# Perceiver block on one core: keys stacked ahead of the output's write, tail weights in five groups, three tail stages at earlier steps, a tanh gate and Newton norms

## The reference

```python
x = x + xattn(layernorm(x), ctx_1024)   # 16 heads of 16, softmax over 4096 keys, projections Wq Wk Wv Wh
x = x + attn(layernorm(x))              # causal linear attention: q, k normalised per head of 16,
                                        # exp features (2 nodes of 32), output projection Wout
x = x + ffn(layernorm(x))               # h = silu(x @ wg.T) * (x @ wu.T); h @ wd.T; hidden 768
# the int32 weights wg, wu, wd are scaled by 1/127
# head norm: x / max(norm(x), 1e-12); layernorm: (x - mean) / sqrt(var + 1e-5)
```

## Time and profile before

| | before |
|---|---|
| median of 3 runs | 1024.28 us (1021.52 to 1024.69) |
| the profiled execution | 1023.58 us |
| its span, first to last instruction | 1021.9 us |
| PE busy | 891.8 us, 87% |
| ACT busy | 546.9 us, 54% |
| DVE busy | 497.6 us, 49% |
| POOL busy | 111.9 us, 11% |
| DMA moved | 118.00 MB, mean 115 GB/s |
| mean granted TensorE clock | 0.958 |
| part of the span before the last scores | 904 us |

### The profile page before, as it was taken

The page is one execution under the profiler, slowest core; times in us unless marked ns, Lnnn a source line. Parts: engine busy times, 40 slices in busy tenths (PEclk is TensorE's granted clock), DMA queues, the critical chain, the costliest instruction groups (busy, mean ns, idle before and its releaser), DMA issues.

```text
span 1021.9 us, 20838 instructions
## 1 busy us (share of the span) xinstructions
PE 891.8 (87%) x8819; PEld 619.7 (61%) x8819; DVE 497.6 (49%) x831; ACT 546.9 (54%) x597; POOL 111.9 (11%) x132
## 2 busy tenths in 40 slices
PE   5699699977999898898899898989899999977865
PEld 4566466645666666665566665665566666656654
DVE  6523135553544346764544345765454445614546
ACT  6177477755565655646465655646466566820101
POOL 1042000000231100000140100000041000004210
PEclk9799899999999999999899999999899999999798
DMA  6898998796866666377866666386967565120000
GB/s 173 147 198 234 154 150 182 146 165 87 173 125 118 111 115 114 101 116 114 187 111 118 107 121 119 89 135 106 180 105 128 103 114 102 14 42 1 1 1 13
DMA packets 59282, 118.00 MB, mean 115 GB/s; under 512 B 23152, under 2 KB 30320, under 8 KB 55728
## 3 DMA queue, kind: packets, MB, share of 16 engines
q1 hardware_dynamic: 57392, 112.22, 60.1%
q0 software_dynamic: 1792, 4.40, 1.5%
HBM read 78.84 MB, written 37.75 MB: 114 GB/s over the span
## 4 chain that ended last, share of the span: by engine, by line
PE 59%; DVE 12%; DMA 11%; issue 6%; ACT 5%; SPq 3%; DVEq 2%; POOL 2%; POOLq 0%; ACTq 0%
PE ps_o L712 16%; PE ps_s L724 12%; PE ps_p L563 7%; PE ps_p L530 7%; DMA kstack<-kscr 7%; ACT probs L993 4%; PE ps_a L656 3%; DVE kfeat L1238 2%; SPq L376 2%; PE ps_a L682 2%; PE ps_a L650 2%; DMA kscr<-kparts 2%; DMA qstack<-qscr 2%; PE ps_a L669 2%; PE ps_a L593 1%
## 5 line engine op out<-in xcount | busy, mean ns | idle before, releaser
L993 ACT ACTIVATE probs<-ps_s 128x1024 f32<-128x1024 f32 x512 | 495.6, 1024 | 289.6 <-PE ps_s L724 266.7
L712 PE MATMUL ps_o<-probs,values 128*17 128x256 f32 x4096 | 258.5, 388 | 0.0
L724 PE MATMUL ps_s<-qstack,kstack 64*128 64x256 f32 x2048 | 206.3, 315 | 56.5 <-DMA kstack<-kscr 34.0
L724 PEld LDWEIGHTS ps_s<-qstack,kstack 64*128 64x128 f32 x2048 | 145.0, 191 | 160.9 <-ACT probs L993 66.5
L712 PEld LDWEIGHTS ps_o<-probs,values 128*17 128x17 f32 x4096 | 106.9, 98 | 95.6 <-issue 12.1
L1030 DVE TENSOR_SCALAR kparts<-ps_p,b_heads 128x512 fp32r<-128x512 f32 x64 | 48.0, 750 | 101.8 <-PE ps_p L530 101.7
L563 PE MATMUL ps_p<-wv_hi,ctx_hi 128*128 128x256 f32 x256 | 79.5, 310 | 1.7 <-DVE wv_lo L1018 1.6
L968 ACT ACTIVATE feat<-feat,node_neg 128x512 f32<-128x512 f32 x32 | 23.1, 722 | 106.9 <-DVE feat L1222 106.9
L1047 DVE TENSOR_TENSOR values<-ps_p,bv_pair 128x512 f32<-128x512 f32 x64 | 44.1, 690 | 66.2 <-PE ps_p L563 66.0
L563 PE MATMUL ps_p<-wv_hi,ctx_lo 128*128 128x256 f32 x256 | 73.0, 285 | 0.0
L563 PE MATMUL ps_p<-wv_lo,ctx_hi 128*128 128x256 f32 x256 | 73.0, 285 | 0.0
(11 more groups left out here) (213 smaller groups left out, 1030.5 us busy)
## 6 DMA issues: line engine op xcount, KB each, us to landing
kstack<-kscr SPq DMA_DIRECT2D x192, 256.0 KB, 9.5
kscr<-kparts SPq DMA_DIRECT2D x64, 512.0 KB, 3.1
ctx_raw<-ctxT SPq DMA_DIRECT2D x32, 512.0 KB, 13.5
qstack<-qscr SPq DMA_DIRECT2D x24, 128.0 KB, 5.2
qscr<-qparts SPq DMA_DIRECT2D x4, 512.0 KB, 3.9
xh<-x SPq DMA_DIRECT2D x4, 256.0 KB, 12.5
xs<-x SPq DMA_DIRECT2D x4, 256.0 KB, 3.7
oscr<-y SPq DMA_DIRECT2D x8, 128.0 KB, 3.6
```

The lines of the kernel that those rows point to most:

```text
L712: last = mm(ps_o[32 * j:32 * j + DH + 1, g * S:(g + 1) * S], values[par][:, i, head_of_step(g, j), :], prob[:, j * S:(j + 1) * S], start=b ...
L724: last = mm(ps_s[s % 2][:, j * S:(j + 1) * S], kstack[par][rows, u, i * P:(i + 1) * P], queries[rows, u, :], start=True, stop=True)
L993: nc.scalar.activation(probs[n % AHEAD][:, :], ps_s[n % 2][:, :], ACT.Exp, scale=float(DH) ** -0.5).then_inc(fast["exp_done"], 1)
```

## The change

- SP: in the first pass of a batch the keys of the next chunk are stacked first; `load_x` and `write_output` come after, and `regroup_output` follows at once.
- POOL: the weight loads are in five groups. Each group waits until one more chunk's keys are stacked: Wh and Wout with the biases and nodes (chunk 1), Wqkv and omega (chunk 2), wg (3), wu (4), wd (5). `setup_tail` on DVE moves from slot 0 to slot 10 of pass 5.
- Steps: y2T from 92 to 91, wout from 93 to 92, ln2T from 98 to 96, gate3 from 114 to 113.
- Gate: ACT computes tanh(g/254) in place of the exponential, and DVE one operation, (tanh + 1) times the product; the factor 1/2 goes into the last scale.
- Head norms: the stages ss0 and ss1 compute 1/sqrt on DVE with an integer seed and three Newton steps (ten operations with a drain between), and POOL's two powers are gone.

```diff
-SETUP_PASS = 5
+SETUP_STEP = 5 * STEPS + 10
-      "o2T0": 88, "o2T1": 89, "y2T": 92, "wout": 93, "ln2T": 98, "gu0": 99, "gate0": 100, "gu1": 101, "gate1": 104,
-      "gu2": 105, "gate2": 108, "gu3": 109, "gate3": 114, "gu4": 115, "gate4": 116, "gu5": 117, "gate5": 120,
+      "o2T0": 88, "o2T1": 89, "y2T": 91, "wout": 92, "ln2T": 96, "gu0": 99, "gate0": 100, "gu1": 101, "gate1": 104,
+      "gu2": 105, "gate2": 108, "gu3": 109, "gate3": 113, "gu4": 115, "gate4": 116, "gu5": 117, "gate5": 120,
...
-            "powered": (["ln0"], ["wh", "norm0", "norm1", "wout"]),
+            "powered": (["ln0"], ["wh", "wout"]),
...
+                    if q + 1 < B * NCH:
+                        stack_keys(fast, q + 1, 1 - p % 2, (fast["scores"], q * STEPS) if q else None)
                     if p == 0 and b:
...
                         write_output(fast, tail_of(b - 1))
-                    if q + 1 < B * NCH:
-                        stack_keys(fast, q + 1, 1 - p % 2, (fast["scores"], q * STEPS) if q else None)
-                    if p == 0 and b:
                         regroup_output(fast, b - 1)
...
-            for dst, src in ((wh_sb, whT), (wout_sb, wout), (wqkv_sb, wqkv)):
+            for dst, src in ((wh_sb, whT), (wout_sb, wout)):
...
+            pool.wait_ge(fast["k_stacked"][0], 2 * STACKED)
+            pool.dma_start(wqkv_sb[:, :, :], wr(wqkv)).then_inc(late_in, 16)
...
+            pool.wait_ge(fast["k_stacked"][1], 2 * STACKED)
             pool.dma_start(wg_int, wr(wgT)).then_inc(i_in, 16)
+            pool.wait_ge(fast["k_stacked"][0], 3 * STACKED)
...
+            pool.wait_ge(fast["k_stacked"][1], 3 * STACKED)
             pool.dma_start(wd_sb[:, :, :].bitcast(INT32), wr(wdT)).then_inc(i_in, 16)
...
-                    nc.scalar.activation(gate_e[:, k % 2, :], bank[:, 0:S], ACT.Exp, scale=-QUANT)
+                    nc.scalar.activation(gate_e[:, k % 2, :], bank[:, 0:S], ACT.Tanh, scale=QUANT / 2)
...
+            def inverse_root(r, a, t):
+
+                v.tensor_scalar(r.bitcast(INT32), a.bitcast(INT32), -0.5, ROOT_SEED, ALU.mult, ALU.add)
+                for _ in range(ROOT_STEPS):
+                    dve.drain()
+                    v.scalar_tensor_tensor(t, a, -0.5, r, ALU.mult, ALU.mult)
+                    dve.drain()
+                    v.tensor_tensor(t, t, r, ALU.mult)
+                    dve.drain()
+                    last = v.scalar_tensor_tensor(r, t, 1.5, r, ALU.add, ALU.mult)
+                return last
...
-                    v.tensor_scalar(ss[:, n, :], ss[:, n, :], 1e-24, None, ALU.max).then_inc(c["variance"], 1)
-                    dve.sem_inc(c["operand"], 1)
-                    return
+                    v.tensor_scalar(ss[:, n, :], ss[:, n, :], 1e-24, None, ALU.max)
+                    dve.drain()
+                    last = inverse_root(rnorm[:, n, :], ss[:, n, :], sq[:, 0:2 * H])
                 elif kind == "norm":
-                    dve.wait_ge(c["powered"], c.at("powered", clock, name))
...
-                    e = gate_e[:, n % 2, :]
-                    v.tensor_scalar(e, e, 1.0, None, ALU.add)
-                    dve.drain()
-                    v.reciprocal(e, e)
-                    dve.drain()
-                    last = v.tensor_tensor(hid[:, n, :], hid[:, n, :], e, ALU.mult)
+                    last = v.scalar_tensor_tensor(hid[:, n, :], gate_e[:, n % 2, :], 1.0, hid[:, n, :],
+                                                  ALU.add, ALU.mult)
...
-                                                  QUANT ** 3, xs[:, :, :], ALU.mult, ALU.add)
+                                                  QUANT ** 3 / 2, xs[:, :, :], ALU.mult, ALU.add)
```

More of the change, by code:

```diff
@@ L33 @@
 EPS = 1e-5
+ROOT_SEED, ROOT_STEPS = float(0x5F3759DF), 3
 QUANT = 1.0 / 127.0
@@ L933, in stage @@
                     masked(c, FEATS.index(name), clock)
-                elif name in ("ln0", "wh", "norm0", "norm1", "wout"):
+                elif name in ("ln0", "wh", "wout"):
                     power(c, name, clock)
@@ L1325, in fast_slot @@
                 q = b * NCH + p
-                if b == 0 and p == SETUP_PASS and s == 0:
+                if q * STEPS + s == SETUP_STEP:
                     setup_tail()
```

12 lines of the change are left out of this document (3 added, 9 removed).

## The result

| | before | after |
|---|---|---|
| median | 1023.55 us (1021.52 to 1024.69, 4 runs) | 997.27 us (996.31 to 999.79, 4 runs) |
| after / before | | 0.9749, 95% interval 0.9723 to 0.9775 |
| the profiled execution, its span | 1023.58, 1021.9 | 996.31, 994.6 |
| mean granted TensorE clock | 0.958 | 0.970 |

The change saves 26 us. The forecast was 985 in a range of 978 to 997, so the direction was right, the gain was 26 where 39 was forecast, and the time lies 0.3 above the upper end.

What follows compares the result with a forecast made beforehand. The prediction took PE, busy 87% of the span, to set the pace, with 34.0 us of waits for stacked keys its largest loss. Terms summed to -39.2 from 1023.58, giving 984.4, forecast as 985, range 978 to 997.

Steps and rivals of the forecast that it cites:

- Weights (-9.4): Batch 0: grouped weight loads remove the 8.4 us key wait and 1.0 us of slow restart; bound 0.
- the keys' write at its usual landing in every pass of batch 0: Sign expected in the profile after: without bunched weight loads, the keys' write lands in its usual 3.1 us.
- The rival of full DMA engines: Batch 0: DMA is busy through most passes, so stalls are spread, not removed; 994 us, chance 0.12.
- Stack first (-22.6 and +2): Batch boundaries: three key waits and slow restarts go, -22.6 us; late output and context cost +2, bounds 0 and +20.
- So it lands near 480 to 481: Batch boundary: the output's write, issued at 469.25 behind the stack, lands when the stack has landed.
- in time in batch 1: Second passes: output's read and context arrive about 1 us late in batches 2 and 3, but not late in batch 1.
- the first rival: Boundary wait returns behind the output's write; sign: context wait ending over 5 us into second pass; 995 to 1005, chance 0.13.
- Gates (-5.0, -9.9): Shorter DVE gates: PE's waits for maxima in the batches go, -5.0 us; last tail's down products come sooner, -9.9.
- Newton norms (0, +2.0): Last tail 0, between -2 and +1; in the batches PE waits 0.65 us three times, +2.0, between 0 and +5.
- norm1 starts within 0.1 us: Last tail: with the new serial DVE chain, norm1 starts within 0.1 us of its earlier place, so the term is 0.
- Earlier steps (+3.7): PE waits 1.5 us at y2T, 0.4 won back at x_lo: +1.1, +1.1, +1.5; bounds -3 and +6.
- ACT's tables: Rival: tanh lies outside the table loaded for exp, so gates cost table loads, 54 us; 1039 us, chance 0.03.

Runs made afterwards that it cites:

- experiment 1: The changed kernel with the output's write issued ahead of the key stacking again, as before the change: 1001.59 us, 0.9782 of before.
- experiment 2: The changed kernel with the context load issued straight behind the key stack, ahead of x and the output's write: 990.68 us, 0.9661 of before.
- experiment 5: The changed kernel with the stack cut in two at a batch's start, x and the output's write between the halves: 988.07 us, 0.9606 of before.
- experiment 9: The cut-stack kernel of experiment 5 with the load of x moved behind the stack's second half: 981.48 us, 0.9592 of before.
- experiment 4: The changed kernel with y2T, wout and ln2T back at steps 92, 93 and 98: 999.89 us, 0.9734 of before.
- experiment 6: The changed kernel with all weight loads behind the first key stack again, casts still at slot 10: 1009.98 us, 0.9854 of before.
- experiment 7: The changed kernel with the head norms computed by POOL's power again: 993.95 us, 0.9709 of before.
- experiment 8: The changed kernel with the gate as exponential, addition, reciprocal and multiplication again: 1017.8 us, 0.9905 of before.
- experiment 3: The changed kernel with the output's write in the batches issued by ACT on its own queue: 1010.75 us, 0.9892 of before.

## Why the prediction was wrong, point by point

**Weights (-9.4).** Right in mechanism and size, within the spread of batch 0. The stall is gone in this profile, -8.0 at once and -8.7 by the end of the batch, and putting it back costs 10.6 to 12.5. In the nine experiments that keep the groups batch 1 starts from 3.2 us sooner to 7.7 later than here, so the size of the gain is known no better. One sign of the prediction failed, "the keys' write at its usual landing in every pass of batch 0": between 60 and 190 us the first of each pass's two writes takes 6.1 to 9.6 us. The 3.1 of the earlier trace rows is a median over the whole kernel; before the change, too, that write took 5.8 to 7.0 in the passes from 131 us on, without any weights. The rival of full DMA engines had this part right; the stack's slack hides it.

**Stack first (-22.6 and +2).** The -22.6 was right as a wait: 21.0 are there at the start of the second passes. The step that failed is "So it lands near 480 to 481" and what hangs on it, up to "Term: +2", the price of what is late next. It measured +15.5, and 17.8 against second passes without such waits. By the keys' write as the zero, the forecast had the stack in at 16, the output at 19, and its read and the context at 22.4 to 24.4; in the trace of batch 2 it was 18.35, 22.8, 26.15 and 27.4. Before the change the last two had been at 27.1 and 28.4. Five things in it were wrong:

- The removed stall was priced as if nothing else came due at its end. The rows of the kernel before already spoke against it: the context issued at 476.44, with the 13.9 us of the earlier trace rows, lands near 490, just behind the end of the stall at 488.18. A PE that comes 7 us sooner has to wait for it unless the context comes 7 us sooner as well, and nothing in the change does that.
- 9.5 is the median over transfers that land one after another, six to a stack. A stack is usable with its last, 12.9 after its issue here. That could be read before, too: the last transfer of the stack in the earlier trace rows is issued near 475.5 and PE's wait for it ends at 488.18.
- The issue of the output's write was taken at its 1.35 us. Behind a stack it took 11.37 and SP was held; the write landed 4.5 us behind the stack, and its read and the context could be issued only then.
- The slack was counted from where DVE splits the context to where PE wants values. But DVE takes yT behind the split, so a late context stops yT and wh, early in the pass; "in time in batch 1" fell by this too (2.31 us of wait).
- What comes after such a wait runs slowly: the eight products of wh took 3.28, 3.57 and 3.78 us, and 1.99 elsewhere, at the lower clock shown above. The forecast counted this for the waits it removed and not for those that it added.

So the first rival (chance 0.13, 995 to 1005) is what happened, with some three quarters of the three waits back (15.5 of 20). Its mechanism was named, with both late pieces, and one of its signs came true in every batch: DVE's wait for the context ended 5.2, 7.2 and 8.4 us into the second pass, where 5 had been named as the mark. The forecast gave it too small a chance, and took its price at 2. Experiments 1, 2, 5 and 9 show it: the loss goes away with the order, moves with the context load, and nearly vanishes when output and context land 4 to 6 us sooner than in the kernel before. In the five profiles that keep SP's order (the changed kernel and experiments 4, 6, 7 and 8) PE's waits for `xT` and `y<-oscr` in the batches come to 10.3 to 15.2 us, so they are no accident of one execution.

**Gates (-5.0, -9.9).** Right in mechanism and place. Measured -6.9 in the batches and -10.0 in the tail by experiment 8, together 2 more than forecast. The batches' part is the four waits for the maxima, 5.0 us, about 1.1 that PE lost beside them, and one wait of 0.8 for the last gate of batch 2's tail. Pace in the tail 1.96 a gate where 1.8 was forecast.

**Newton norms (0, +2.0).** In the batches 2.3 by the waits and 3.2 by experiment 7: within the bounds. In the last tail "norm1 starts within 0.1 us" held (0.01), but the term of 0 did not: it is +2.3, just beyond the +1 given. The ten operations (917.21 to 919.88, 2.67 us) stand ahead of the first transposes, so PE sat idle for 5.64, up to 927.03, and then ran at half clock. The windows after, from 926 and from 933 (window, length, busy of five engines, granted clock, DMA share, GB/s):

```profile
926.00:933.00 7.00, 5.97 (x30) 5.81 (x30) 2.26 (x4) 0.00 (x0) 0.00 (x0) 0.55 0.00 0
933.00:945.00 12.00, 8.74 (x56) 7.12 (x56) 6.66 (x11) 2.29 (x4) 3.51 (x6) 1.00 0.01 1
```

0.55 is mostly the lower of its two levels, 1.2 GHz, and the 22 warm-up products took 4.70 us there and 2.62 in the kernel before. The length of the idle stretch alone does not decide this: in experiment 7 they took 4.05 behind 2.06 us of idle, in the kernel before 2.62 behind the same 2.06. The products stand ahead of the second transposes, whose result comes 2.7 later than before, counted from the last exponential. All of this was won back further on, by luck: not by anything that the edit does but by the clock, which in experiment 7 was high there too: the eight products of the features took 1.99 where they took 3.78 before, and those of wout 1.99 where they took 3.64. That is why the last tail gained 11.8 with 10.0 from the gates and 2.3 lost to the norms (the other 4 are the clock's), and why only experiment 7 shows the price.

**Earlier steps (+3.7).** Right: +5.1 at y2T less 1.6 behind it, +3.6. The wait was forecast at 1.5 and was

```profile
376.02 0.66 PE L585 MATMUL ps_a<-ident,y 128*128 128x128 f32 x4 [1.48 <-DVE y L1096]
```

and the one for `x_lo` stayed at 2.9, as forecast.

**ACT's tables.** The one table load of the trace stays the only one, so tanh is in the set that was loaded for exp, and this rival is out. The Trainium skill, page "ScalarE: Activation LUTs", section "Table sets: the hidden batching unit", says so, and the trace agrees.

**Sum.** The forecast sum is -39.2 and the profiled executions differ by -27.3, so 11.9 are missing. By the table of passes, measured less forecast: weights +0.7; start of batch 1 -0.6; boundaries with the norms -3.2 against -22.6 + 2 + 2.0 = -18.6, so +15.4; earlier steps -0.1; gates in the batches -1.9; last tail -11.8 against -9.9, so -1.9; small pieces +0.3. Together +11.9. One term is more than the whole of the error; the gates' extra in the batches and the tail's, which is the clock's, hid 3.8 of it.

**The clock in pass 6.** The steps of about 1.5 us that come and go in pass 6 go with the granted clock behind its wait of 2.9 us for `x_lo`. Among kernels with the new steps the pass takes 30.8 us at a mean of 1.00 (batch 2 of experiments 1, 3 and 9, batch 1 of 2; 31.2 in batch 1 of 7), 32.3 to 32.4 at 0.947 (both batches of the changed kernel) and 33.5 at 0.90 (batch 2 of experiment 2). Why it is high or low behind the same wait stays open.

**What stays open.** Why the issue of the output's write takes 3 to 13 us behind a stack is not explained. The traces narrow it down: in the changed kernel and all experiments but 1 there are 27 such held issues, and every one ended 0.0 to 1.0 us before the last transfer ahead of it landed (0.4 in the three of the changed kernel). That it waits for room in a queue fits this, but no run here measured the room. The variation of the key waits in batch 0 was not looked into.

## What to carry to other kernels

Before a removed stall is booked in full, look in the old trace for what else lands near its end; here the output's read and the context landed 0.5 and 1.8 us behind it, and the earlier PE had to wait for them instead. When a transfer is moved in front of another, cost the other one by the last landing of all that is now ahead of it and by its issue in that place, then follow each engine's own order from it to the first consumer; here that was a split that stood in front of a copy, not the values it was for. If both transfers are urgent, cut the larger one around the smaller: this gave back 9.6 of the 15.5 us, and 15.0 with the load of x moved behind both (experiments 5 and 9). And a serial chain moved from a slow engine to a busy one should be priced at the place where its first half was needed, not at its last.

## What the hardware showed that was not expected

- The issue of the output's write (two transfers of 128 KB) takes 1.35 us with nothing in front, 4.24 behind three stack transfers and x, 11.37 behind six and x, and 13.29 behind six, a context load and x, on SP; on ACT it took 11.10 behind six and x, and the engine computed nothing for 10.18. All 27 issues that were held so ended 0.0 to 1.0 us before the last transfer ahead of them landed.
- Six stack transfers of 256 KB issued within 2.65 us land 2.1 us apart, not together.
- Around the end of an idle stretch of 5.64 us, from 926 to 933, PE's granted clock was 0.55, and the same 22 products took 4.70 us in place of 2.62; in the kernel before, the low stretch (0.54, from 945 to 956) fell on the features instead.
- One pass of the same work took 30.8, 32.3 or 33.5 us, at a mean granted clock of 1.00, 0.947 or 0.90.
